# Moving one low-part subtraction from VectorE to GpSimd in the first group of a batched graph-attention kernel, and the point from which GpSimd's first sum may start

## The chip, the cores and the metric

The kernel runs on one core of one Trainium2 chip. The metric is the device time of one execution in microseconds (us). It was run three times before the change: 520.58, 521.08 and 521.65 us, median 521.08 us. The profile comes from a further execution that took 520.78 us.

## The reference, cut to what matters

For each of 32 batches, x is 256 x 512 and adj is 256 x 256; `weight`, `wq` and `wk` are 512 x 512 and shared by all batches.

```
output = x @ weight
q, k   = x @ wq, x @ wk
alpha  = max(q @ k^T, 0) * (adj != 0)
alpha  = softmax(alpha, axis=1)
out    = layernorm(x + alpha @ output)
```

All of it is float32.

## The kernel before, in words

**Splits.** TensorE multiplies a float32 matrix in three passes: each operand X is kept as a high part (`X_hi`, X rounded to the type TensorE reads) and a low part (`X_lo = X - X_hi`), and a product is hi·hi + lo·hi + hi·lo. `add_chunk` (lines 339 to 341) issues these three matmuls. ScalarE makes the high parts by a copy; VectorE or GpSimd makes the low parts by a subtraction.

**Algebra.** The score matrix is x (wq wk^T) x^T, so the kernel first computes G = wq wk^T once, and then for every batch T = G x^T, the scores from x and T, V = x W, and the softmax-weighted sum of V. T and V are made with a Strassen-like scheme of seven half-size products P1 to P7. Their left operands are the four blocks A11, A12, A21, A22 of x and four sums of blocks S1 to S4; their right operands are blocks of G (or W) and four sums T1, T2, T3, D4 of such blocks.

**Order of the work.** The batches go in pairs (16 of them), the pairs in groups of two called slot 0 and slot 1. `x_summed`, `s_hi_ready` and `s_lo_ready` are semaphores with one counter per slot. Groups 1 to 7 run in a rolled loop; the first group (pairs 0 and 1) is written out by hand, as are the queues of all engines. Each engine executes its own list strictly in order, so a waiting instruction holds all that stands behind it.

**The first group on TensorE** runs: 14 warm-up matmuls, `fill_g` (G), `fill_first_v` for three of four rows of V of pair 0, then `fill_first_t` (T of both pairs, products in the order P1, P2, P7, P6, P5, P3, P4, two halves each of six matmuls), the scores of pair 0 in two halves (`fill_first_s`), the last row of V, the scores of pair 1, and so on. `fill_first_v(0)` waits for the low parts of all four rows of W (`w_lo_ready`, count K = 4). P6 multiplies S2 by T2: it waits for the low part of T2 of G (`gt_lo_ready`, made by `split_gt(T2)` on VectorE), for the low part of S2 in both slots, and for the first copy of the chain bank. P5 waits for T1 and S1, P3 for S4. P3's first half also waits for ScalarE's copy of P5's first half (`t_copied` 5), and ScalarE's `copy_first_t(P5, 0)` in turn waits until GpSimd has made the low part of A22 of slot 1.

**VectorE in this stretch** makes the low parts of x of pair 0 (`split_x0`, four), of W (four), then the splits and sums of G, among them `split_first_s(0, S3)`, `split_first_b(A11)`, `split_first_b(A12)`, `split_first_s(1, S3)`, `split_gt(T3)`, `split_first_s(0, S2)`, `split_first_s(1, S2)`, `split_gt(T2)`, `split_first_v(2)`, `split_gt(T1)`, two sums of A11 and `split_gt(D4)`. The subtractions are all recorded at line 1110 (the helper `rest`).

**GpSimd in this stretch** makes the block sums S1 to S4 of both slots (`sum_first_x`, recorded at line 1527), the low parts of S1 and S4 of both slots (`split_first_s`, line 1531), the low parts of A22 and A21 of slot 1 (`split_first_a`, line 1536), and then the four sums of blocks of W (lines 1614 to 1622). Its first sum waits for the low parts of wq and wk, the second for `w_lo_ready`. Pair 0's sums lie in `xs`; pair 1's lie in parts of `parts` and `adj`, and SyncE loads the first adjacency matrix over the latter once the sums and low parts of S1 and S4 of slot 1 are done.

**ScalarE** makes the high parts in the order of its list: the high part of S3 of slot 0 (line 1000) stands directly behind the third split of G and ahead of A11 (line 993), the fourth split of G and `split_first_v(0)` (line 971).

Of the kernel before, what the change touches and what calls it, by code (L numbers as in the profile page):

```python
# [38 lines left out]
S1, S2, S3, S4 = range(4)  # L39
# [6 lines left out]
S_HI = ({S2: 1, S3: 2, S1: 3, S4: 4}, {S3: 1, S2: 2, S4: 3, S1: 4})  # L46
S_LO = ({S2: 1, S3: 2, S1: 3, S4: 4}, {S3: 1, S2: 2, S1: 3, S4: 4})

FIRST_A, FIRST_S = (A11, A12, A22, A21), (S3, S1, S2, S4)
FIRST_LO = {S3: 1, S2: 2}, {S1: 1, S4: 2}  # L50

T_HI = ({A11: 1, A22: 2, A12: 3, A21: 4}, {A11: 1, A12: 2, A21: 3, A22: 4})
T_LO = ({A11: 1, A22: 2, A12: 3, A21: 4}, {A11: 1, A12: 2, A22: 3, A21: 4})
# [12 lines left out]
def gnn_resnorm(nc: bass.Bass, x, x_t, adj_t, w, wq_t, wk_t, out):  # L66
# [3 lines left out]
    K = D // P  # L70
# [10 lines left out]
    with ExitStack() as ctx:  # L81
# [107 lines left out]
        w_hi_ready, w_lo_ready = sem("w_hi_ready"), sem("w_lo_ready")  # L189
# [8 lines left out]
        x_summed, s_hi_ready, s_lo_ready = sems("x_summed"), sems("s_hi_ready"), sems("s_lo_ready")  # L198
# [138 lines left out]
        def _(pe):  # L337
# [38 lines left out]
            def fill_t(i):  # L376
                def copy_taken(n):
                    pe.wait_ge(t_copied, COPIES * i + n)

                def sum_taken(n):  # L380
                    pe.wait_ge(t_summed, T_SUMS * i + n)

                def x_split(u):
                    pe.wait_ge(a_lo_ready[0], 4 * i + A_LO[0][u])
                    if u in B_LO_FIRST:
                        pe.wait_ge(b_lo_ready, 2 * i + B_LO_FIRST[u])
                    else:
                        pe.wait_ge(a_lo_ready[1], 2 * i + A_LO[1][u])

                def xs_split(s):  # L390
                    for slot in range(2):
                        pe.wait_ge(s_lo_ready[slot], 4 * i - 2 + S_LO[slot][s])

                both = slice(0, 2)
                xs_split(S3)
                t_half(P7, 0, both)

                pe.wait_ge(v_lo_ready, 8 * i - 4 + V_AT[1][A12])
                x_split(A11)
                t_half(P1, 0, both)  # L400
                t_half(P1, 1, both)

                pe.wait_ge(v_summed, V_SUMS * (2 * i - 2) + 2)
                x_split(A12)
                t_half(P2, 0, both)
                pe.wait_ge(v_summed, V_SUMS * (2 * i - 2) + 3)
                t_half(P7, 1, both)
                sum_taken(1)
                t_half(P2, 1, both)
                copy_taken(1)  # L410
                xs_split(S2)
                t_half(P6, 0, both)
                copy_taken(2)
                t_half(P6, 1, both)
                copy_taken(3)
                xs_split(S1)
                t_half(P5, 0, both)
                copy_taken(4)
                t_half(P5, 1, both)
                copy_taken(5)  # L420
                xs_split(S4)
                t_half(P3, 0, both)
                copy_taken(6)
                t_half(P3, 1, both)
                sum_taken(3)
                x_split(A22)
                t_half(P4, 0, both)
                sum_taken(4)
                t_half(P4, 1, both)

            def fill_first_t():

                def xs_split(s):
                    for slot in range(2):
                        if s in FIRST_LO[0]:
                            pe.wait_ge(first_s_lo_ready[slot], FIRST_LO[0][s])
                        else:
                            pe.wait_ge(s_lo_ready[slot], FIRST_LO[1][s])

                both = slice(0, 2)  # L440
                pe.wait_ge(g_lo_ready, 2)
                pe.wait_ge(b_lo_ready, B_LO_FIRST[A11])
                t_half(P1, 0, both)
                t_half(P1, 1, both)
                pe.wait_ge(g_lo_ready, 4)
                pe.wait_ge(gt_summed, 1)
                pe.wait_ge(b_lo_ready, B_LO_FIRST[A12])
                t_half(P2, 0, both)

                pe.wait_ge(v_lo_ready, 2)  # L450
                t_half(P2, 1, both, o_bank[0][:])
                pe.wait_ge(gt_lo_ready, G_ORDER.index(T3) + 1)
                xs_split(S3)

                pe.wait_ge(v_lo_ready, 1)
                t_half(P7, 0, both)

                pe.wait_ge(gt_summed, 8)
                t_half(P7, 1, both)
                pe.wait_ge(t_copied, 1)  # L460
                pe.wait_ge(gt_lo_ready, G_ORDER.index(T2) + 1)
                xs_split(S2)
                t_half(P6, 0, both)
                pe.wait_ge(t_copied, 2)
                t_half(P6, 1, both)
                pe.wait_ge(t_copied, 3)
                pe.wait_ge(gt_lo_ready, G_ORDER.index(T1) + 1)
                xs_split(S1)
                t_half(P5, 0, both)
                pe.wait_ge(t_copied, 4)  # L470
                t_half(P5, 1, both)
                pe.wait_ge(t_copied, 5)
                xs_split(S4)
                t_half(P3, 0, both)
                pe.wait_ge(t_copied, 6)
                t_half(P3, 1, both)
                pe.wait_ge(t_summed, 3)
                pe.wait_ge(gt_lo_ready, G_ORDER.index(D4) + 1)
                pe.wait_ge(a_lo_ready[1], A_LO[1][A22])
                t_half(P4, 0, both)  # L480
                pe.wait_ge(t_summed, 4)
                t_half(P4, 1, both)
# [625 lines left out]
        def _(dve):  # L1108
# [237 lines left out]
            def split_first_s(slot, s):  # L1346
                dve.wait_ge(s_hi_ready[slot], FIRST_S.index(s) + 1)
                rest(s_lo[:, slot, s], xs[:, s] if slot == 0 else xs1_raw[s], s_hi[:, slot, s]).then_inc(first_s_lo_ready[slot], 1)
# [48 lines left out]
            sum_gt(D4, 1)  # L1397
            split_first_v(1)
            split_gt(T3)
            split_first_s(0, S2)  # L1400
            split_first_s(1, S2)
            split_gt(T2)
            split_first_v(2)
# [106 lines left out]
        @block.gpsimd  # L1510
        def _(pool):
            def first_sum_split(slot, s):
                if s in FIRST_LO[0]:
                    pool.wait_ge(first_s_lo_ready[slot], FIRST_LO[0][s])
                else:
                    pool.wait_ge(s_lo_ready[slot], FIRST_LO[1][s])

            def sum_first_x(slot, s):
                xb = {u: xt[:, u] for u in range(4)} if slot == 0 else x1_raw
                xs_to = {u: xs[:, u] for u in range(4)} if slot == 0 else xs1_raw  # L1520
                for u in {S3: (A11, A21), S1: (A22,), S2: (), S4: (A12,)}[s]:
                    pool.wait_ge((x0_loaded if slot == 0 else x1_loaded)[u], 16)
                if s in (S2, S4):
                    pool.wait_ge(x_summed[slot], S_SUMMED[s] - 1)
                a, b, op = {S3: (xb[A11], xb[A21], ALU.subtract), S1: (xb[A21], xb[A22], ALU.add),
                            S2: (xs_to[S1], xb[A11], ALU.subtract), S4: (xb[A12], xs_to[S2], ALU.subtract)}[s]
                nc.gpsimd.tensor_tensor(xs_to[s], a, b, op).then_inc(x_summed[slot], 1)

            def split_first_s(slot, s):
                pool.wait_ge(s_hi_ready[slot], FIRST_S.index(s) + 1)  # L1530
                nc.gpsimd.tensor_tensor(s_lo[:, slot, s], xs[:, s] if slot == 0 else xs1_raw[s], s_hi[:, slot, s].bitcast(F32),
                                        ALU.subtract).then_inc(s_lo_ready[slot], 1)
# [6 lines left out]
            def sum_x(i, slot, s, first=False):  # L1539
                for u in {S3: (A11, A21), S1: (A22,), S2: (), S4: (A12,)}[s]:  # L1540
                    pool.wait_ge(xt_loaded[u], 32 * i + 16 * slot - 16)

                if not first:
                    pool.wait_ge(s_lo_ready[1 - slot], 4 * i - 6 + 4 * slot + S_LO[1 - slot][s])
                else:
                    first_sum_split(0, s)
                if s in (S2, S4):
                    pool.wait_ge(x_summed[slot], 4 * i + S_SUMMED[s] - 1)
                a, b, op = {S3: (xt[:, A11], xt[:, A21], ALU.subtract), S1: (xt[:, A21], xt[:, A22], ALU.add),
                            S2: (xs[:, S1], xt[:, A11], ALU.subtract), S4: (xt[:, A12], xs[:, S2], ALU.subtract)}[s]  # L1550
                nc.gpsimd.tensor_tensor(xs[:, s], a, b, op).then_inc(x_summed[slot], 1)  # L1551
# [40 lines left out]
            nc.gpsimd.memset(minus_half[:], -0.5).then_inc(half_ready, 1)  # L1592
            pool.wait_ge(half_ready, 1)

            pool.wait_ge(qk_lo_ready, 2 * K)
            sum_first_x(0, S3)

            pool.wait_ge(w_lo_ready, K)
            sum_first_x(0, S1)
            sum_first_x(1, S3)  # L1600
            sum_first_x(0, S2)
            sum_first_x(1, S1)
            sum_first_x(1, S2)
            split_first_s(0, S1)
            split_first_s(1, S1)
            sum_first_x(0, S4)
# [79 lines left out]
```

## Time and profile before

| what | value |
|---|---|
| runs before, us | 520.58, 521.08, 521.65 (median 521.08) |
| profiled execution, us | 520.78 |
| its span, us | 519.0 |
| granted TensorE clock, mean over the span | 0.997 of full |
| TensorE busy | 98% of the span |
| VectorE, ScalarE, GpSimd busy | 73%, 64%, 51% |

The span is the time from the first to the last instruction of the profiled execution; the remaining 1.78 us of it lie around the span. Times in the rows are counted from the start of the span. PE is TensorE's matmuls, PEld its weight loads, DVE is VectorE, ACT is ScalarE, POOL is GpSimd, SPq is SyncE's queue, which issues DMAs. A matmul's duration overlaps its follower's, so the pace of TensorE is read from the distance of two starts.

### The profile page before, as it was taken

To read this page: it belongs to the slowest core of one execution; us is meant where nothing else is said; L and a number is where in the kernel's file an instruction comes from. 1 tells how busy PE (TensorE), PEld (TensorE's weight loads), DVE (VectorE), ACT (ScalarE), POOL (GpSimd) and SP (SyncE) were. 2 spreads that over 40 slices of the span, in tenths; PEclk is the share of its full clock that TensorE was granted. 3 is DMA by queue.
4 is the path that set the end of the run, shared out by engine and by line. 5 is a ranking of instruction groups with operands and counts; after the bars stand their busy time and mean duration, and the time that the engine had idled before them with its cause. 6 is when DMAs were issued, how large, how long until landed. Compare 5 with 4: busy or idle time off the path is not lost.

```text
span 519.0 us, 9822 instructions
## 1 busy us (share of the span) xinstructions
PE 510.6 (98%) x3206; PEld 464.0 (89%) x3206; DVE 379.1 (73%) x744; ACT 330.9 (64%) x756; POOL 263.4 (51%) x199
## 2 busy tenths in 40 slices
PE   8999999999999999999999999999999999999995
PEld 7779998899989998899988999889998999889994
DVE  6997855776848677586866778577684866757586
ACT  6855756386763857649474586638676385764677
POOL 1799884339535377145651486433953537610011
PEclk9999999999999999999999999999999999999998
DMA  8412151044520626025350342405342061501426
GB/s 291 175 61 83 67 182 58 20 124 163 178 84 20 221 62 242 20 61 182 116 203 20 125 139 110 175 20 151 132 179 84 20 222 61 202 1 35 168 90 235
DMA packets 30367, 62.05 MB, mean 120 GB/s; under 512 B 2064, under 2 KB 2320, under 8 KB 30352
## 3 DMA queue, kind: packets, MB, share of 16 engines
q1 hardware_dynamic: 30064, 61.48, 34.7%
q10 hardware_dynamic: 288, 0.39, 0.2%
q8 instruction: 7, 0.11, 0.1%
q14 instruction: 8, 0.07, 0.0%
HBM read 45.09 MB, written 16.78 MB: 119 GB/s over the span
## 4 chain that ended last, share of the span: by engine, by line
PE 95%; DMA 1%; SPq 1%; DVE 1%; issue 1%; ACT 0%; POOLq 0%; POOL 0%; DVEq 0%; ACTq 0%
PE o_bank L339 12%; PE o_bank L340 12%; PE o_bank L341 12%; PE chain L339 11%; PE chain L341 11%; PE chain L340 11%; PE bank_y L339 6%; PE bank_y L340 6%; PE bank_y L341 6%; PE bank_z L341 3%; PE bank_z L340 3%; PE bank_z L339 3%; DMA xn<-in_w 1%; SPq L293 0%; SPq L289 0%
## 5 line engine op out<-in xcount | busy, mean ns | idle before, releaser
L1560 POOL TENSOR_TENSOR s_lo<-xs,s_hi 128x512 fp32r<-128x512 f32 x56 | 76.4, 1378 | 36.7 <-ACT s_hi L727 36.7
L1555 POOL TENSOR_TENSOR a_lo<-xt,a_hi 128x512 fp32r<-128x512 f32 x42 | 57.5, 1375 | 61.3 <-ACT a_hi L719 61.3
L339 PE MATMUL o_bank<-t_hi,a_hi 128*128 128x256 f32 x256 | 72.5, 283 | 0.0
L340 PE MATMUL o_bank<-t_lo,a_hi 128*128 128x256 f32 x256 | 72.4, 283 | 0.0
L341 PE MATMUL o_bank<-t_hi,a_lo 128*128 128x256 f32 x256 | 72.4, 283 | 0.0
L1565 POOL TENSOR_TENSOR rstd<-var_eps,minus_half 128x4 f32<-128x4 f32 x14 | 14.2, 1017 | 92.6 <-DVE var_eps L1202 92.6
L750 ACT COPY parts<-chain 128x256 f32<-128x256 f32 x90 | 33.2, 369 | 43.3 <-PE chain L341 42.1
L1122 DVE TENSOR_TENSOR parts<-parts,bank_y 128x512 f32<-128x512 f32 x32 | 22.0, 688 | 41.9 <-ACT parts L736 25.8
L1551 POOL TENSOR_TENSOR xs<-xt 128x512 f32<-128x512 f32 x28 | 36.8, 1325 | 27.9 <-DMA xt<-in_x_t 27.9
L339 PE MATMUL chain<-w_hi,s_hi 128*128 128x256 f32 x180 | 50.9, 283 | 0.0
L340 PE MATMUL chain<-w_lo,s_hi 128*128 128x256 f32 x180 | 50.9, 283 | 0.0
L341 PE MATMUL chain<-w_hi,s_lo 128*128 128x256 f32 x180 | 50.9, 283 | 0.0
L1188 DVE SCALAR_TENSOR_TENSOR xn<-o_bank,xn 128x512 f32<-128x512 f32 x62 | 42.4, 684 | 10.2 <-PE o_bank L341 10.1
L339 PEld LDWEIGHTS o_bank<-t_hi,a_hi 128*128 128x128 f32 x256 | 49.1, 192 | 0.4
L340 PEld LDWEIGHTS o_bank<-t_lo,a_hi 128*128 128x128 f32 x256 | 49.1, 192 | 0.4
L341 PEld LDWEIGHTS o_bank<-t_hi,a_lo 128*128 128x128 f32 x256 | 49.1, 192 | 0.0
L339 PE MATMUL o_bank<-v_hi,p_hi 128*128 128x512 f32 (+1 forms) x126 | 49.0, 389 | 0.1
L340 PE MATMUL o_bank<-v_lo,p_hi 128*128 128x512 f32 (+1 forms) x126 | 48.9, 388 | 0.0
L341 PE MATMUL o_bank<-v_hi,p_lo 128*128 128x512 f32 (+1 forms) x126 | 48.8, 387 | 0.0
L1110 DVE TENSOR_TENSOR v_lo<-parts,v_hi 128x512 fp32r<-128x512 f32 x45 | 46.8, 1052 | 0.1
L1208 DVE TENSOR_SCALAR xn<-xn,neg_mean,rstd 128x512 f32<-128x512 f32 x56 | 39.3, 723 | 10.1 <-POOL rstd L1565 10.1
L778 ACT CAST t_hi<-parts 128x512 fp32r<-128x512 f32 x24 | 14.8, 621 | 49.8 <-PE o_bank L341 49.8
(209 smaller groups left out, 1648.6 us busy)
## 6 DMA issues: line engine op xcount, KB each, us to landing
xn<-in_x SPq DMA_DIRECT2D x16, 1024.0 KB, 5.2
xt<-in_x_t SPq DMA_DIRECT2D x60, 256.0 KB, 3.1
out<-xn SPq DMA_DIRECT2D x14, 1024.0 KB, 5.3
adj<-in_adj_t SPq DMA_DIRECT2D x16, 512.0 KB, 4.8
xn<-in_wq_t SPq DMA_DIRECT2D x4, 256.0 KB, 4.0
xn<-in_w SPq DMA_DIRECT2D x4, 256.0 KB, 6.9
out<-xn SPq DMA_DIRECT2D x2, 512.0 KB, 3.1
parts<-in_wk_t SPq DMA_DIRECT2D x3, 256.0 KB, 4.5
```

The lines of the kernel that those rows point to most:

```text
L339: nc.tensor.matmul(dst, a[0], b[0], start=first, stop=False, skip_group_check=shared)
L340: nc.tensor.matmul(dst, a[0], b[1], start=False, stop=False, skip_group_check=shared)
L341: return nc.tensor.matmul(dst, a[1], b[0], start=False, stop=last, skip_group_check=shared)
L750: nc.scalar.copy(parts[:, PART[product], c, 0], chain_v[:, c]).then_inc(v_copied, 1)
L778: nc.scalar.copy(t_hi[:, u], whole).then_inc(t_hi_ready, 1)
L1110: return nc.vector.tensor_tensor(dst, whole, hi.bitcast(F32), ALU.subtract)
L1122: nc.vector.tensor_tensor(part, part, bank, ALU.add).then_inc(t_summed, 1)
L1188: nc.vector.scalar_tensor_tensor(out=xn[:, slot, r], in0=row.rearrange("q j n -> q (j n)"), scalar=1.0, in1=xn[:, slot, r], op0=ALU.mult, ...
L1208: nc.vector.tensor_scalar(xn[:, slot, r], xn[:, slot, r], neg_mean[:, r:r + 1], rstd[:, r:r + 1], ALU.add, ALU.mult).then_inc(normed, 1)
L1551: nc.gpsimd.tensor_tensor(xs[:, s], a, b, op).then_inc(x_summed[slot], 1)
L1555: nc.gpsimd.tensor_tensor(a_lo[:, slot, u], xt[:, u], a_hi[:, slot, u].bitcast(F32), ALU.subtract).then_inc(a_lo_ready[slot], 1)
L1560: nc.gpsimd.tensor_tensor(s_lo[:, slot, s], xs[:, s], s_hi[:, slot, s].bitcast(F32), ALU.subtract).then_inc(s_lo_ready[slot], 1)
```

## The change: what it does

- VectorE no longer makes the low part of S2 of slot 0 (`split_first_s(0, S2)` leaves its list). GpSimd makes it, behind its sum S2 of slot 1 and ahead of its low part of S1 of slot 0.
- GpSimd's wait for the low parts of W stands ahead of its first sum (S3 of slot 0) and no longer behind it; the wait for the low parts of wq and wk goes.
- The counts follow: in slot 0 GpSimd now signals three low parts in the first group and VectorE one; `S_LO_LESS` corrects the counts that the loop waits for.

```diff
-FIRST_LO = {S3: 1, S2: 2}, {S1: 1, S4: 2}
+FIRST_LO_DVE = {S3: 1}, {S3: 1, S2: 2}
+FIRST_LO_POOL = {S2: 1, S1: 2, S4: 3}, {S1: 1, S4: 2}
+
+S_LO_LESS = (1, 2)
...
-                        pe.wait_ge(s_lo_ready[slot], 4 * i - 2 + S_LO[slot][s])
+                        pe.wait_ge(s_lo_ready[slot], 4 * i - S_LO_LESS[slot] + S_LO[slot][s])
...
-                        if s in FIRST_LO[0]:
-                            pe.wait_ge(first_s_lo_ready[slot], FIRST_LO[0][s])
+                        if s in FIRST_LO_DVE[slot]:
+                            pe.wait_ge(first_s_lo_ready[slot], FIRST_LO_DVE[slot][s])
                         else:
-                            pe.wait_ge(s_lo_ready[slot], FIRST_LO[1][s])
+                            pe.wait_ge(s_lo_ready[slot], FIRST_LO_POOL[slot][s])
...
             split_gt(T3)
-            split_first_s(0, S2)
             split_first_s(1, S2)
             split_gt(T2)
...
                 if not first:
-                    pool.wait_ge(s_lo_ready[1 - slot], 4 * i - 6 + 4 * slot + S_LO[1 - slot][s])
+                    pool.wait_ge(s_lo_ready[1 - slot],
+                                 4 * (i - 1 + slot) - S_LO_LESS[1 - slot] + S_LO[1 - slot][s])
...
-            pool.wait_ge(qk_lo_ready, 2 * K)
+            pool.wait_ge(w_lo_ready, K)
             sum_first_x(0, S3)
-
-            pool.wait_ge(w_lo_ready, K)
             sum_first_x(0, S1)
             sum_first_x(1, S3)
             sum_first_x(0, S2)
             sum_first_x(1, S1)
             sum_first_x(1, S2)
+            split_first_s(0, S2)
             split_first_s(0, S1)
             split_first_s(1, S1)
```

## Rows read from the trace of the kernel before

**Rows 1.** The page, busy time and share of the span by engine.

```profile
PE 510.6 (98%) x3206; PEld 464.0 (89%) x3206; DVE 379.1 (73%) x744; ACT 330.9 (64%) x756; POOL 263.4 (51%) x199
```

**Rows 2.** Windows: length, then PE, PEld, DVE, ACT, POOL busy, PE's clock, DMA.

```profile
16.50:17.50 1.00, 0.90 (x5) 0.43 (x4) 1.00 (x3) 1.00 (x4) 0.41 (x1) 1.00 0.15 57
17.50:33.00 15.50, 15.50 (x70) 12.82 (x69) 15.50 (x21) 11.17 (x22) 15.42 (x11) 1.00 0.21 69
33.00:35.00 2.00, 0.82 (x5) 0.39 (x4) 2.00 (x3) 0.00 (x0) 2.00 (x2) 1.00 0.00 0
49.50:507.00 457.50, 457.50 (x2958) 419.72 (x2958) 330.87 (x670) 292.08 (x685) 227.56 (x170) 1.00 0.33 113
```

**Rows 3.** Timeline of PE: start us, duration us, line, operation, idle time before.

```profile
16.57 0.39 PE L341 MATMUL bank_y<-s_hi,t_lo 128*128 128x512 f32 x1
17.06 0.50 PE L339 MATMUL bank_y<-w_hi,a_hi 128*128 128x512 f32 x1
17.40 0.39 PE L340 MATMUL bank_y<-w_lo,a_hi 128*128 128x512 f32 x1
...
33.29 0.39 PE L341 MATMUL bank_y<-s_hi,g_lo 128*128 128x512 f32 x1
34.86 0.47 PE L339 MATMUL chain<-s_hi,g_hi 128*128 128x512 f32 x1 [1.18 <-issue]
35.17 0.39 PE L340 MATMUL chain<-s_lo,g_hi 128*128 128x512 f32 x1
...
48.61 0.28 PE L341 MATMUL o_bank<-t_hi,a_lo 128*128 128x256 f32 x1
48.75 0.39 PE L339 MATMUL o_bank<-t_hi,a_hi 128*128 128x256 f32 x1
48.98 0.28 PE L340 MATMUL o_bank<-t_lo,a_hi 128*128 128x256 f32 x1
```

**Rows 4.** The chain that ended last, in order of time: start, duration, engine.

```profile
14.82 0.62 ACT w_hi L1017
...
16.33 0.69 DVE w_lo L1110
```

**Rows 5.** Timeline of DVE.

```profile
29.59 1.78 DVE L1110 TENSOR_TENSOR s_lo<-xs,s_hi 128x512 fp32r<-128x512 f32 x1
31.29 1.78 DVE L1110 TENSOR_TENSOR s_lo<-parts,s_hi 128x512 fp32r<-128x512 f32 x1
33.00 1.76 DVE L1110 TENSOR_TENSOR g_lo<-xn,g_hi 128x512 fp32r<-128x512 f32 x1
34.68 0.68 DVE L1110 TENSOR_TENSOR v_lo<-o_bank,v_hi 128x512 fp32r<-128x512 f32 x1
...
47.51 1.19 DVE L1110 TENSOR_TENSOR t_lo<-parts,t_hi 128x512 fp32r<-128x512 f32 x1 [0.69 <-ACT t_hi L762]
```

**Rows 6.** Timeline of POOL.

```profile
11.72 1.72 POOL L1527 TENSOR_TENSOR xs<-xt 128x512 f32<-128x512 f32 x1 [10.89 <-DMA xt<-in_x_t]
17.09 1.30 POOL L1527 TENSOR_TENSOR xs<-xt 128x512 f32<-128x512 f32 x1 [3.64 <-DVE w_lo L1110]
18.35 1.29 POOL L1527 TENSOR_TENSOR parts<-soft 128x512 f32<-128x512 f32 x1
...
24.38 1.79 POOL L1531 TENSOR_TENSOR s_lo<-xs,s_hi 128x512 fp32r<-128x512 f32 x1
...
34.17 1.73 POOL L1536 TENSOR_TENSOR a_lo<-parts,a_hi 128x512 fp32r<-128x512 f32 x1
...
46.85 1.30 POOL L1551 TENSOR_TENSOR xs<-xs,xt 128x512 f32<-128x512 f32 x1
```

**Rows 7.** DVE from 12.24 us on, in narrow windows of the timeline.

```profile
12.24 1.76 DVE L1110 TENSOR_TENSOR a_lo<-xt,a_hi 128x512 fp32r<-128x512 f32 x1
```

**Rows 8.** Timeline of ACT.

```profile
20.12 0.59 ACT L971 CAST v_hi<-bank_y 128x512 fp32r<-128x512 f32 x1 [1.56 <-PE bank_y L341]
...
39.34 0.59 ACT L745 COPY parts<-chain 128x512 f32<-128x512 f32 x1 [0.33 <-PE chain L341]
```

**Rows 9.** Timeline of SP.

```profile
34.28 0.33 SPq L307 DMA_DIRECT2D adj<-in_adj_t  x1
```

**Rows 10.** Timeline of DVE, the first mask.

```profile
49.03 0.69 DVE L1161 SCALAR_TENSOR_TENSOR soft<-adj,o_bank 128x512 f32<-128x512 int32 x1 [0.33 <-PE o_bank L341]
```

More of the change, by code:

```diff
@@ L1512, in first_sum_split @@
             def first_sum_split(slot, s):
-                if s in FIRST_LO[0]:
-                    pool.wait_ge(first_s_lo_ready[slot], FIRST_LO[0][s])
+                if s in FIRST_LO_DVE[slot]:
+                    pool.wait_ge(first_s_lo_ready[slot], FIRST_LO_DVE[slot][s])
                 else:
-                    pool.wait_ge(s_lo_ready[slot], FIRST_LO[1][s])
+                    pool.wait_ge(s_lo_ready[slot], FIRST_LO_POOL[slot][s])
             def sum_first_x(slot, s):
```

## The prediction

> **What bounds the kernel now.** I read the page first: TensorE is busy for 98% of the span, every other engine for 73% or less [rows 1]. So a microsecond is worth something only where TensorE stands still. The windows show where: TensorE is busy without a break from 49.5 to 507 us and from 17.5 to 33.0, but has only 0.82 of the 2.00 us from 33 to 35, and 0.90 of the one at 16.5 [rows 2]. The granted clock is 1.00 in all four, so no level of the clock is at stake.
>
> The timeline of TensorE gives the prices. Undisturbed, matmuls on 512 columns start 0.227 us apart (from 17.40 to 33.29 are 70 steps, 15.89 us; the count is that of the second window [rows 2]). Three places break the pace [rows 3]:
> - At 16.57 the last matmul of G starts. The next two are due at 16.80 and 17.02 and come at 17.06 and 17.40: **0.38 us** lost, wait and restart together.
> - At 33.29 the last matmul of P7 starts. The next two are due at 33.52 and 33.74 and come at 34.86 and 35.17: **1.43 us** lost.
> - At 48.61, on 256 columns with a pace of 0.12, the two behind it come at 48.75 and 48.98 instead of 48.73 and 48.85: **0.13 us** lost.
>
> Who ends them? For the first, the chain names VectorE's last low part of W, 16.33 to 17.02 [rows 4]. The second is labelled "issue", which names nobody; but P6 waits for the low part of T2, and VectorE makes that from 33.00 to 34.76 [rows 5], 0.10 before P6 starts. The third waits for the low part of T's block A21, which ends at 48.70 [rows 5].
>
> The rows also show why VectorE is late. A subtraction whose operands are all in SBUF takes 1.76 to 1.78 us, one with its operand in a PSUM bank (34.68) takes 0.68 [rows 5]. GpSimd's instructions show the mirror image: 1.30 us at 17.09, 1.72 to 1.79 at 11.72, 24.38 and 34.17 [rows 6]. The two alternate: where both queues are full, each pair takes 1.70 us (distance of starts 29.59, 31.29, 33.00), about 1.15 for GpSimd and 0.55 for VectorE. So an SBUF subtraction costs VectorE 1.70 us of its queue here, and adds 0.45 to GpSimd, whose own pace is 1.26 (17.09 to 18.35).
>
> **Part 1: the first sum waits.** GpSimd's sum at 11.72 runs beside VectorE's four low parts of x; the third of those, at 12.24, takes 1.76 [rows 7] where 0.68 would do. With the sum gone from there the four end 1.1 us earlier. VectorE's low parts of W then follow ScalarE, whose last high part of W ends at 14.82 + 0.62 = 15.44 [rows 4]. The last low part runs from about 15.47 to 16.15 instead of 16.33 to 17.02: 0.87 earlier. TensorE needs it at 16.80, so the first stall goes whole: **minus 0.38**. What is late next: nothing, G itself paces TensorE. ScalarE now has to wait for S3: GpSimd starts it at about 16.23, it ends at 17.53, and ScalarE's high part of S3 stood ready for it at 16.9. ScalarE so loses 0.65 us, covered by its idle 1.56 before the high part of V at 20.12 [rows 8], which comes 0.38 earlier itself: 0.5 is left over. Cost 0. No DMA is issued earlier or later by this but those below.
>
> **Part 2: VectorE's queue.** The low part of T2 is the eighth SBUF subtraction of VectorE behind W and becomes the seventh. From 34.76 go 1.70 for the one removed and 0.87 for the earlier start: 32.2. TensorE wants P6 at 33.52 - 0.38 = 33.14, so T2 must land by 33.04. It does, by 0.8: **minus 1.43**. The rows leave one doubt. Which engine goes first when both are ready within 0.05 us decides whether VectorE waits for one GpSimd instruction more, 1.15 us, and my walk meets three such ties (about 23.5, 27.0 and 28.0). One lost tie puts T2 at 33.3, P6 at 33.4, and takes back 0.2 plus a restart of 0.08. I take none lost, as the nearest rows alternate evenly; 0.28 is the bound for the range.
>
> **Part 3: GpSimd's queue.** It takes two instructions more behind 16.23. Check of the price on before: from 17.09 to 35.90, the end of A22's low part (34.17 + 1.73), 12 instructions and 8 alternations, 12 x 1.26 + 8 x 0.45 = 18.7 against 18.8 measured. After: 14 instructions, 8 or 9 alternations, 21.2 to 21.7 us, so A22 ends at 37.5 to 37.9, 1.6 to 2.0 later than before. Who waits for what stands in that queue:
> - S2's low part itself, now seventh, ends at 16.23 + 7 x 1.26 + 4 x 0.45 = 26.9; P6 wants it at 33.14. Free.
> - The low part of S4 of slot 1 ends at about 36.2; P3 wants it at 38.6. The adjacency load behind it on SyncE, issued at 34.28 [rows 9], moves to 36.3; the mask that needs it runs at 49.03 [rows 10]. Free; the load behind it waits for later events.
> - A22: ScalarE's copy of P5's first half, at 39.34 [rows 8] and due at 37.5 after the shift, waits for it. P3 is 24 steps behind P6, at 33.14 + 5.45 = 38.6. If A22 ends at 37.9, the copy (0.59 long) ends at 38.55. Free, but only just; 0.1 at the bound.
> - The sums of W and what follows come 1 to 1.5 us later. ScalarE's splits of W have 3 us of cover. But they lie differently beside VectorE: the low part of A21 of T, at 47.51, waited there for a GpSimd instruction that ran 46.85 to 48.15 [rows 5, 6]. Free it would take 0.68 and end 0.5 early; behind a GpSimd instruction just begun it ends 0.6 late. Today it costs 0.13. The bounds are 0 and 0.7, I take **0.28, which is 0.15** more than today, since GpSimd is busy there without a break.
>
> **Sum.** 0.38 + 1.43 - 0.15 = 1.66 us. From 49.5 us on TensorE has no idle stretch [rows 2] and the other engines follow it, so the whole shift reaches the end. The profiled execution would go from 520.78 to 519.12. It lies 0.30 below the median of the runs, so against the median 521.08 the sum gives 519.4; half of the ties' 0.28 is a fair allowance, and I say 519.5. A measurement of this kernel can tell about 0.2%, 1.04 us, from no change.
>
> **A rule against the change.** VectorE's subtraction alone takes 0.68 us, GpSimd's alone 1.30 [rows 5, 6]. The Trainium skill (GPSIMD Engine Reference, Engine selection) sends elementwise work on a tile to VectorE and calls GpSimd about twice as slow with two inputs. By that rule the move swaps a cheap instruction for one of twice its price; the trace agrees on the bare ratio, 1.9. The sum goes by the 1.70 us of queue instead, because both queues are full there.
>
> **The rivals.**
> 1. *VectorE gains only the bare price.* If the removed subtraction is worth its pace alone, 0.60, and the earlier start is eaten by the later sums, T2 lands at 34.16 and P6 starts at 34.26: 0.60 plus 0.38 gained, less 0.15. Gain 0.8, 520.3. Against it stand the 1.70 steps. Chance 0.07.
> 2. *The ties fall badly.* 0.28 lost at P6, 0.1 at P3, and 0.7 instead of 0.13 at 48.7: 1.81 - 0.28 - 0.1 - 0.57 = 0.86, 520.2; with two of the three, gain 1.1. For it: nothing fixes the phases. Chance 0.20, half of it under 1.04 us.
> 3. *Slower: GpSimd's queue becomes the bound.* Place: ScalarE's copy of P5's first half behind A22's low part. P3 then starts 0.69 after A22 ends, so it costs from 37.9 on and eats the whole gain from 39.7 on. If all 14 instructions take the 1.79 of 24.38, A22 ends at 41.3, P3 is 3.4 late, and the kernel is 1.6 slower: 522.7. Against it: VectorE has only nine SBUF subtractions in that time. Chance 0.05.
> 4. *It does not do what it says*: P6 is held by something else ("issue" names nobody), and only the first stall goes: 520.7. Against it: the 0.10 between T2's end and P6. Chance 0.05.
>
> **How the numbers follow.** Forecast, a gain of 1.2 to 1.95: 0.60. Rivals 0.07, 0.20, 0.05, 0.05; 0.03 is left for small gains of other kinds. Faster by over 0.2%: 0.60 + 0.10 = 0.70. Within: 0.07 + 0.10 + 0.05 + 0.03 = 0.25. Slower 0.05. Range: below, a gain of 1.94 (no third stall at all) and 0.3 for the scatter of the runs, 518.9; above, rivals 1 and 2 with the same scatter, 520.6. It leaves out rivals 3 and 4.
>
> **What would show it.** Right: TensorE steps evenly through 16.8; VectorE's last low part of W starts near 15.5; T2 ends at 32 to 33.1; no gap in TensorE ahead of P6; A22's low part ends before 38; scores of pair 0 start near 44.1 instead of 45.86. Wrong: T2 ends behind 33.1, a gap ahead of P3 near 38.6, or one of over 0.5 us between the two halves of the scores near 47.

## The result, and the profile after

The changed kernel is slower: 523.93 us (median of 7 runs, 522.59 to 524.51) against 521.04 us (7 runs) of the kernel before, ratio 1.005 with an interval of 1.0036 to 1.0065. The forecast was 519.5, range 518.9 to 520.6. The profiled execution has a span of 522.6 us against 519.0.

The stall ahead of P6 is gone. V starts 0.54 us earlier, though behind a longer stall (0.80 us against 0.38), and two small new stalls came; all that is over by 48 us. What decides comes later. The timeline of TensorE after the change (start, duration, line, operation, idle time before), to be held against [rows 3]:

```profile
15.60 0.39 PE L345 MATMUL bank_y<-s_hi,t_lo 128*128 128x512 f32 x1
16.52 0.50 PE L343 MATMUL bank_y<-w_hi,a_hi 128*128 128x512 f32 x1 [0.53 <-DVE w_lo L1114]
...
35.47 0.39 PE L345 MATMUL chain<-s_hi,g_lo 128*128 128x512 f32 x1
35.97 0.50 PE L343 MATMUL chain<-s_hi,g_hi 128*128 128x512 f32 x1
...
38.59 0.39 PE L345 MATMUL chain<-s_hi,g_lo 128*128 128x512 f32 x1
39.20 0.50 PE L343 MATMUL chain<-s_hi,g_hi 128*128 128x512 f32 x1 [0.21 <-ACT parts L749]
...
58.95 0.28 PE L345 MATMUL o_bank<-t_hi,a_lo 128*128 128x256 f32 x1
62.17 0.50 PE L343 MATMUL o_bank<-v_hi,p_hi 128*128 128x512 f32 x1 [2.94 <-DVE v_lo L1114]
62.51 0.39 PE L344 MATMUL o_bank<-v_lo,p_hi 128*128 128x512 f32 x1
62.74 0.45 PE L345 MATMUL o_bank<-v_hi,p_lo 128*128 128x512 f32 x1
62.99 0.63 PE L343 MATMUL o_bank<-v_hi,p_hi 128*128 128x512 f32 x1
63.42 0.63 PE L344 MATMUL o_bank<-v_lo,p_hi 128*128 128x512 f32 x1
```

Between 58.95 and 62.17 TensorE waits 3.1 us for the low part of V's last row. Then its matmuls stand 0.43 apart instead of 0.23. The windows (length, busy time of PE, PEld, DVE, ACT, POOL, then the granted clock) say that this is the clock, granted at 0.81 and then at 0.50 of full:

```profile
59.10:62.20 3.10, 0.15 (x3) 0.03 (x1) 3.10 (x4) 1.53 (x3) 3.10 (x3) 1.00 0.00 0
62.20:63.40 1.20, 1.20 (x4) 0.98 (x5) 1.20 (x3) 0.00 (x0) 1.20 (x2) 0.81 0.00 0
63.40:66.00 2.60, 2.60 (x8) 2.01 (x7) 1.88 (x10) 1.09 (x4) 2.60 (x3) 0.50 0.52 162
70.00:510.00 440.00, 440.00 (x2845) 403.76 (x2845) 314.88 (x633) 279.70 (x654) 212.28 (x157) 1.00 0.33 113
```

In the first two of these windows VectorE and GpSimd are both busy without a break. VectorE after the change, the four low parts of P of pair 0 (line 1182) and then the one that TensorE waits for:

```profile
54.12 1.69 DVE L1114 TENSOR_TENSOR t_lo<-parts,t_hi 128x512 fp32r<-128x512 f32 x1
55.74 1.52 DVE L1182 SCALAR_TENSOR_TENSOR p_lo<-soft,inv_sum,p_hi 128x256 fp32r<-128x256 f32 x1
57.18 1.52 DVE L1182 SCALAR_TENSOR_TENSOR p_lo<-soft,inv_sum,p_hi 128x256 fp32r<-128x256 f32 x1
58.62 1.50 DVE L1182 SCALAR_TENSOR_TENSOR p_lo<-soft,inv_sum,p_hi 128x256 fp32r<-128x256 f32 x1
60.04 1.48 DVE L1182 SCALAR_TENSOR_TENSOR p_lo<-soft,inv_sum,p_hi 128x256 fp32r<-128x256 f32 x1
61.44 0.68 DVE L1114 TENSOR_TENSOR v_lo<-o_bank,v_hi 128x512 fp32r<-128x512 f32 x1
```

The same instructions in the kernel before, which the prediction did not read:

```profile
55.08 0.66 DVE L1110 TENSOR_TENSOR t_lo<-parts,t_hi 128x512 fp32r<-128x512 f32 x1
55.87 1.30 DVE L1178 SCALAR_TENSOR_TENSOR p_lo<-soft,inv_sum,p_hi 128x256 fp32r<-128x256 f32 x1
57.10 0.47 DVE L1178 SCALAR_TENSOR_TENSOR p_lo<-soft,inv_sum,p_hi 128x256 fp32r<-128x256 f32 x1
57.49 0.47 DVE L1178 SCALAR_TENSOR_TENSOR p_lo<-soft,inv_sum,p_hi 128x256 fp32r<-128x256 f32 x1
57.89 0.47 DVE L1178 SCALAR_TENSOR_TENSOR p_lo<-soft,inv_sum,p_hi 128x256 fp32r<-128x256 f32 x1
58.29 0.68 DVE L1110 TENSOR_TENSOR v_lo<-o_bank,v_hi 128x512 fp32r<-128x512 f32 x1
```

GpSimd beside them, in the kernel before:

```profile
52.77 1.75 POOL L1625 TENSOR_TENSOR w_lo<-xn,w_hi 128x512 fp32r<-128x512 f32 x1
55.42 1.46 POOL L1560 TENSOR_TENSOR s_lo<-xs,s_hi 128x512 fp32r<-128x512 f32 x1 [0.90 <-ACT s_hi L727]
58.03 1.50 POOL L1560 TENSOR_TENSOR s_lo<-xs,s_hi 128x512 fp32r<-128x512 f32 x1 [1.14 <-ACT s_hi L727]
```

and after the change:

```profile
55.23 1.75 POOL L1628 TENSOR_TENSOR w_lo<-xn,w_hi 128x512 fp32r<-128x512 f32 x1
56.93 1.48 POOL L1564 TENSOR_TENSOR s_lo<-xs,s_hi 128x512 fp32r<-128x512 f32 x1
58.38 1.46 POOL L1564 TENSOR_TENSOR s_lo<-xs,s_hi 128x512 fp32r<-128x512 f32 x1
59.79 1.44 POOL L1628 TENSOR_TENSOR w_lo<-xn,w_hi 128x512 fp32r<-128x512 f32 x1
```

Before, GpSimd stood idle for 0.90 and 1.14 us in this stretch, waiting for ScalarE. In the second pause three of the four low parts of P ran at 0.47 us each. After, GpSimd comes later: its low part of W, the one ahead of the first pause, starts at 55.23 instead of 52.77. TensorE and VectorE come some 1 us earlier (the last matmul ahead of the wait starts at 58.95 instead of 60.11). So both pauses are filled, and each low part of P waits for one GpSimd instruction, at 1.5 us. The four last 5.78 us from start to end instead of 2.49.

The differences add up, with a gap taken as what stands above the pace of 0.227 (0.119 on 256 columns): V starts at 16.52 instead of 17.06, -0.54; P6, -1.42; new ahead of P5, +0.37; new ahead of P3, +0.48; the low part of T's A21, -0.11; the wait near 59, 3.10 and 0.11 for its restart, +3.21; eight matmul steps at the lower clock (62.99 to 66.38), +1.57. Sum +3.56, and the spans differ by 3.6.

### The profile page after: what moved, and what is told of

The parts are those of the page before. It is cut to its first block, busy times and chain, and to the rows that moved or that the text cites. A ratio compares the mean times of both kernels' runs of the same rounds, so it can differ in the third digit from the quotient of the medians.

```text
span 522.6 us, 9802 instructions
## 1 busy us (share of the span) xinstructions
PE 511.9 (98%) x3206; PEld 464.5 (89%) x3206; DVE 380.1 (73%) x743; ACT 331.0 (63%) x756; POOL 267.4 (51%) x200
## 4 chain that ended last, share of the span: by engine, by line
PE 86%; DVE 1%; issue 0%; POOLq 0%; POOL 0%; ACT 0%; DVEq 0%; ACTq 0%
PE o_bank L343 11%; PE o_bank L344 11%; PE o_bank L345 11%; PE chain L344 10%; PE chain L345 10%; PE chain L343 10%; PE bank_y L344 5%; PE bank_y L343 5%; PE bank_y L345 5%; PE bank_z L344 3%; PE bank_z L345 3%; PE bank_z L343 3%; DVE p_lo L1182 0%; DVE xn L1460 0%; DVE xn L1192 0%
## 5 line engine op out<-in xcount | busy, mean ns | idle before, releaser
L1126 DVE TENSOR_TENSOR parts<-parts,bank_y 128x512 f32<-128x512 f32 x32 | 21.9, 687 | 42.6 <-ACT parts L740 25.8
L1114 DVE TENSOR_TENSOR v_lo<-parts,v_hi 128x512 fp32r<-128x512 f32 x45 | 48.8, 1096 | 0.1
L740 ACT COPY parts<-chain 128x512 f32<-128x512 f32 x42 | 24.6, 587 | 34.7 <-PE chain L345 34.2
```

The lines of the kernel that those rows point to most:

```text
L740: nc.scalar.copy(parts[:, PART[product], c], chain[:, c]).then_inc(t_copied, 1)
L1114: return nc.vector.tensor_tensor(dst, whole, hi.bitcast(F32), ALU.subtract)
L1126: nc.vector.tensor_tensor(part, part, bank, ALU.add).then_inc(t_summed, 1)
```

## The experiments

All times are medians of runs beside the kernel before on the same chip, with the ratio and its interval.

**1 and 2: GpSimd holds still during the low parts of P.** In the changed kernel, and as a control in the kernel before.

```diff
             for b in W_ORDER[:-1]:
+                if b == T2:
+                    pool.wait_ge(p_lo_ready, R)
                 split_wt(b)
```

Expected of the first:

> The changed kernel, but GpSimd waits for the low parts of P of pair 0 (p_lo_ready = 4) ahead of its low part of W's T2, so that nothing of GpSimd runs beside those four VectorE instructions. Theory A (GpSimd's queue, moved 1 to 2 us later and without its two idle gaps, runs beside VectorE's four low parts of P and makes each take 1.5 us where 0.68 would do; TensorE then waits for the low part of V's last row, and its clock falls): the four take about 2.5 us in all where they took 5.8, TensorE has no gap near 59 us and no stretch at half clock, and the time is that of before less the 1.1 us gained until then, 519.5 to 520.3. Theory B (the time is lost elsewhere, for instance in the loop or in transfers that start later, and the gap near 59 us is only where it shows): another wait takes the gap's place, 522.5 to 524.5.

Of the control:

> The kernel before with the same hold of GpSimd ahead of its low part of W's T2. Theory A: the four low parts of P take 2.5 us in the kernel before already, so the hold gains nothing; its own cost is nothing either, if GpSimd's later instructions have cover: 520.8 to 521.3. If the hold by itself were worth a microsecond, a good result of the first run would not speak for theory A.

Measured: 523.55 (ratio 1.0054, 1.0033 to 1.0076) and 522.79 (1.0042, 1.0028 to 1.0056). Theory A's time failed in both runs; the first lies in theory B's range, 522.5 to 524.5. The traces say why. The first wait is gone: in run 1 the four low parts of P take 1.66 us from start to end and no gap stands near 59 us. But the hold keeps GpSimd still for 2.22 us (4.81 in the control, where 2.04 were idle before), and TensorE meets GpSimd again at the start of the second group. TensorE in the changed kernel with the hold:

```profile
74.64 0.28 PE L345 MATMUL bank_y<-w_hi,a_lo 128*128 128x256 f32 x1
77.53 0.50 PE L343 MATMUL bank_y<-s_hi,g_hi 128*128 128x512 f32 x1 [2.61 <-POOL s_lo L1564]
```

and GpSimd there:

```profile
68.88 1.29 POOL L1559 TENSOR_TENSOR a_lo<-xt,a_hi 128x512 fp32r<-128x512 f32 x1
70.13 1.30 POOL L1555 TENSOR_TENSOR xs<-xt 128x512 f32<-128x512 f32 x1
...
74.53 1.27 POOL L1555 TENSOR_TENSOR xs<-xt 128x512 f32<-128x512 f32 x1 [3.10 <-DMA xt<-in_x_t]
75.76 1.71 POOL L1564 TENSOR_TENSOR s_lo<-xs,s_hi 128x512 fp32r<-128x512 f32 x1
```

The last low part of x of pair 2 ends at 70.17; the block of pair 3 is loaded over it only then; the sum S1 waits for that load until 74.53; and the low part of S3, which P7 wants, stands behind that sum. So GpSimd's whole queue of the first group has little slack. Another wait took the gap's place, as theory B said, so these two runs do not decide between the theories; run 5 does.

**5 and 6: the low part of S3 goes ahead of the sum that waits**, with the hold and without it.

```diff
             sum_x(1, 1, S3)
-            sum_x(1, 1, S1)
             split_s(1, 1, S3)
+            sum_x(1, 1, S1)
             sum_x(1, 1, S2)
```

> The changed kernel with the hold of the first run, and with GpSimd's low part of S3 of slot 1 for the second group moved ahead of its sum S1 of that slot, which waits for a transfer. Theory A (two places, both GpSimd's queue: the low parts of P near 57 us, and behind the hold the low part of S3 that stands behind the sum waiting for x of pair 3): both gaps go, TensorE has none between 48 and 505 us, and the time is that of before less what was gained until 48 us: 519.8 to 520.5. Theory B (GpSimd's queue is too full anywhere in the first group): a third wait appears in the second group, 521.5 or more.

> The changed kernel with only the low part of S3 moved ahead of the sum S1, without the hold. Theory A: the low parts of P are slowed as before, the wait of 3 us near 59 us stays, and the move is worth nothing there: 522.6 to 524.5, as the changed kernel.

Measured: with the hold 520.07 (ratio 0.9988, 0.9979 to 0.9997), without it 524.42 (1.0067, 1.0052 to 1.0082). With both edits the two waits are gone; only 0.42 us near 81 us stays between 48 and 506, and no third wait of theory B's kind comes. The swap by itself does nothing for the wait near 59 us, which is 3.1 us again. Between 5 and 6 the hold is the only difference, and it is worth over 4 us (524.42 against 520.07). This is what shows that GpSimd's instructions beside the low parts of P cost the time.

**3 and 4: each part of the change alone.** Run 3 keeps the old start of the first sum, run 4 leaves the low part of S2 on VectorE.

```diff
# run 3, against the changed kernel
-            pool.wait_ge(w_lo_ready, K)
+            pool.wait_ge(qk_lo_ready, 2 * K)
             sum_first_x(0, S3)
+
+            pool.wait_ge(w_lo_ready, K)
             sum_first_x(0, S1)
# run 4, against the kernel before: the reverse of these lines
```

> Only the low part of S2 of slot 0 goes to GpSimd; the first sum starts as before, ahead of the low parts of W. Theory A: the low part of T2 ends 1.7 earlier, at 33.1, TensorE is about 1.3 ahead at 50 us, and GpSimd 0.8 behind, which together is as much as its idle 0.90 and 1.14 us near 55 and 57; so most of the four low parts of P are slowed, TensorE waits 1 to 3 us for the last row of V: 520.5 to 523. Theory B: nothing of it near 59 us, 519.7.

> Only the wait moves: GpSimd's first sum starts behind the low parts of W; VectorE keeps the low part of S2. Theory A: both queues start 0.9 earlier, TensorE gains 0.4 at 17 us and up to 0.9 ahead of P6; GpSimd is 0.4 behind, so some 0.4 us of its idle time is left near 55 us, and one or two low parts of P are slowed: TensorE waits 0 to 1.5 us, 519.8 to 521.5. Theory B: 519.8.

Measured: 525.23 (1.0079, 1.0062 to 1.0095) and 524.94 (1.0063, 1.0043 to 1.0082). Each alone is as slow as both. In both traces all four low parts of P take 1.5 us, and TensorE waits over 3 us. Run 4 was expected to wait 1.5 us at most, with GpSimd 0.4 us behind. GpSimd in run 4:

```profile
54.07 1.75 POOL L1623 TENSOR_TENSOR w_lo<-xn,w_hi 128x512 fp32r<-128x512 f32 x1
55.78 1.74 POOL L1560 TENSOR_TENSOR s_lo<-xs,s_hi 128x512 fp32r<-128x512 f32 x1
57.62 1.35 POOL L1560 TENSOR_TENSOR s_lo<-xs,s_hi 128x512 fp32r<-128x512 f32 x1
```

GpSimd was further behind than 0.4. Its first sum starts at 16.63, only 0.46 ahead of where its second stood before, and it meets VectorE once more on the way: its low part of A22 ends at 37.16 instead of 35.90, and its low part of W at 55.82 instead of 54.52, 1.30 later. VectorE's instruction in front of the low parts of P, at 54.67 instead of 55.08, now starts beside that low part of W and takes 1.70 instead of 0.66; by the time the low parts of P come, ScalarE has GpSimd's next operand ready and no pause is left for them. So what was wrong is the size of GpSimd's delay. What a delay of 0.4 us would do, this run does not show. From 1.30 us here to 2.46 in the changed kernel the loss does not grow: TensorE waits 3.1 us in both.

Run 4 also shows that the new wait alone does not help P6: the low part of T2 ends 0.45 earlier, at 34.31, and the stall ahead of P6 is 1.46 us, as long as before. Run 3 also showed what the first sum's early start saves: no stall ahead of P5 or P3, but 0.95 us between 44 and 49 us.

**7 and 8: a dose in the kernel before.** One subtraction more on GpSimd, ahead of the sums of W, 512 or 192 columns wide; its result is overwritten unread. Nothing else is touched.

```diff
+            pool.wait_ge(xt_loaded[A11], 16)
+            pool.wait_ge(xt_loaded[A12], 16)
+            nc.gpsimd.tensor_tensor(p_lo[:, 0:M], xt[:, A11], xt[:, A12], ALU.subtract)
             pool.wait_ge(w_lo_ready, K)
```

> The kernel before with one more subtraction of 128 x 512 on GpSimd, 1.26 us, ahead of its sums of W; its result is read by nobody. Nothing else is changed, VectorE's and TensorE's lists are those of before. Theory A: a GpSimd queue 1.26 us later loses its idle 0.90 us near 55, runs beside the low parts of P without a break, and slows two to four of them from 0.47 to 1.5 us; the last row of V has 1.2 us of slack, so TensorE waits 1 to 2.5 us near 60 us: 522 to 525. Theory B (the loss needs the change's other parts): 521.2.

> The same with 128 x 192, some 0.5 us. Theory A, as a dose: 0.5 us stays within the idle 0.90 us near 55, GpSimd's low part of S2 starts where it did, one low part of P is slowed as before, and the time is that of before: 520.9 to 521.6. If 0.5 us brings the whole wait, the idle time is not what protects the low parts of P.

Measured: 525.48 (1.0087, 1.0072 to 1.0103) and 521.41 (1.0007, 0.9998 to 1.0016). One instruction of 1.26 us on an engine that is busy for half of the span costs 4.6 us; the short one costs nothing that is clear of noise. VectorE with the wide one:

```profile
55.18 1.69 DVE L1110 TENSOR_TENSOR t_lo<-parts,t_hi 128x512 fp32r<-128x512 f32 x1
56.79 1.52 DVE L1178 SCALAR_TENSOR_TENSOR p_lo<-soft,inv_sum,p_hi 128x256 fp32r<-128x256 f32 x1
...
62.50 0.68 DVE L1110 TENSOR_TENSOR v_lo<-o_bank,v_hi 128x512 fp32r<-128x512 f32 x1
```

and with the narrow one:

```profile
55.65 0.66 DVE L1110 TENSOR_TENSOR t_lo<-parts,t_hi 128x512 fp32r<-128x512 f32 x1
56.45 1.30 DVE L1178 SCALAR_TENSOR_TENSOR p_lo<-soft,inv_sum,p_hi 128x256 fp32r<-128x256 f32 x1
57.67 0.47 DVE L1178 SCALAR_TENSOR_TENSOR p_lo<-soft,inv_sum,p_hi 128x256 fp32r<-128x256 f32 x1
```

VectorE's and TensorE's lists are those of the kernel before in both, so in run 7 GpSimd's lateness alone brings the whole effect.

Run 8 is no clean dose. GpSimd's low part of W starts 0.58 us later (53.35), but its pauses stay 0.90 and 1.13 us, although 0.90 less 0.58 would be 0.32. The reason lies ahead of them: VectorE's low part of T's block A21 met a GpSimd instruction just begun, and TensorE lost 0.66 us there instead of 0.13.

```profile
47.54 1.73 DVE L1110 TENSOR_TENSOR t_lo<-parts,t_hi 128x512 fp32r<-128x512 f32 x1 [0.69 <-ACT t_hi L762]
```

TensorE, ScalarE and VectorE then run 0.57 later as well (VectorE's instruction at 55.65 instead of 55.08), so beside them GpSimd is as early as in the kernel before. The run therefore does not show that a delay of half a microsecond is harmless to the low parts of P, and no run here has a delay against VectorE between that of the kernel before and those of runs 4 and 7.

**9 to 11: versions that might beat both.** Run 9 is run 3 with the hold and the swap. Run 10 is run 5 with the hold one instruction later:

```diff
             for b in W_ORDER[:-1]:
                 split_wt(b)
+            pool.wait_ge(p_lo_ready, R)
             split_s(1, 0, S2)
```

Run 11 is run 10 with A22 of slot 1 split earlier on ScalarE and GpSimd.

```diff
# ScalarE
+            split_first_a(A22)
+            split_first_a(A21)
             split_first_s(0, S4)
             split_first_s(1, S4)
-            split_first_a(A22)
-            split_first_a(A21)
# GpSimd
+            split_first_a(A22)
             split_first_s(1, S4)
-            split_first_a(A22)
             split_first_a(A21)
```

> The third run's kernel (only S2's low part moved; the first sum starts ahead of W's low parts) with the hold and the earlier low part of S3. Theory A: no gap near 59 us and none near 75; what stays is the first stall (0.4) and the two at 44 and 47 us (0.2 and 0.7) that the third run showed: 519.9 to 520.6. It tells what the first sum's wait is worth once GpSimd's queue no longer decides.

> As the fifth run, but the hold stands one instruction later, behind the low part of W's T2: GpSimd stands idle for about 1 us instead of 2.2, one or two of the low parts of P run beside it. The last row of V has 1.2 us of slack or more, so TensorE should have no gap near 59 us, and the stall of 0.42 us near 81 us goes if it comes from GpSimd being late: 519.6 to 520.3.

> As the tenth, and A22 and A21 of slot 1 are split earlier: their high parts ahead of those of S4 on ScalarE, where it stood idle for 3 us, and GpSimd's low part of A22 ahead of that of S4 of slot 1. Theory: the stalls of 0.37 and 0.48 us ahead of P5 and P3 come from ScalarE's and GpSimd's late A22; both go or shrink, unless the low part of S4 of slot 1, now last, is late for P3 itself (a stall near 38 us of up to 0.8): 519.0 to 520.0.

Measured: 520.20 (0.9988, 0.9979 to 0.9997), 519.60 (0.9978, 0.9969 to 0.9987) and 519.86 (0.9978, 0.9969 to 0.9987). Run 10 has the lowest median, 1.36 us under the kernel before: nearly the gain that was forecast for the change, had with one more wait and one line moved. Its interval overlaps those of runs 5, 9 and 11, so it is not shown to be better than they are. GpSimd stands still for 1.55 us in it, one low part of P takes 1.51 and no gap comes near 59 us; of the stall near 81 us 0.1 is left. Its windows, TensorE first:

```profile
16.00:48.00 32.00, 31.76 (x154) 26.23 (x153) 27.13 (x36) 19.90 (x39) 31.62 (x21) 1.00 0.28 90
48.00:505.80 457.80, 457.80 (x2960) 419.76 (x2958) 330.95 (x670) 292.72 (x685) 233.57 (x172) 1.00 0.33 113
```

Run 11 took away the stall ahead of P5 and left 0.34 ahead of P3, but TensorE then waited 0.70 us near 47 us for a low part of T; the sum is unchanged. Run 9 against run 5 (ratio 0.9988 in both) says that the first sum's wait is worth nothing that these runs can tell.

## Why the prediction was wrong, step by step

- **What bounds the kernel**: right. TensorE's three stalls and who ends them were read rightly; the low part of T2 held P6, since the stall goes in the changed kernel and in run 3.
- **Part 1**: right in kind, its size varies. The last low part of W ended at 16.46, 0.55 earlier than before and not 0.87. The stall ahead of V is 0.37 to 1.05 us in the six profiles without the new wait (before, runs 2, 3, 7, 8, 9); of the seven with it, it is gone in four (5, 6, 10, 11) and 0.31, 0.56 and 0.80 in the others (4, 1, after). The 0.80 comes with a G that ended 0.97 earlier than before; in that execution ScalarE also waited 0.41 us in the middle of its high parts of x for a load, which it had not done in the profile before.
- **Part 2**: right. T2 was to land at 32.2 and ended at 32.58 (30.81 + 1.77 in the trace); P6 starts without a stall, 1.42 gained for 1.43 forecast. No tie fell badly. The removed subtraction did this alone: run 3 has no stall there either, and run 4 keeps it.
- **Part 3, A22**: a size off. It was to end at 37.5 to 37.9 and ended at 38.48 (the first sum started at 16.60 instead of 16.23, and the 14 instructions took 21.9 us instead of 21.2 to 21.7), so the copy of P5's first half, and with it P3, were late by 0.48; rival 3's place, at a seventh of its price. A second stall, 0.37 ahead of P5, was not foreseen: ScalarE's copies stood behind its high parts of S4 and A22, which waited for GpSimd's sums.
- **Part 3, "the sums of W and what follows"**: this is the step that failed. It followed GpSimd's queue to the low part of T's A21, put 0.15 us down for it, and stopped at 48.7 us; what lies behind was taken at nothing. The measured price of that was 3.21 us of waiting and 1.57 of lower clock in the profile. Seven microseconds on, VectorE has four more instructions with all tensors in SBUF, and GpSimd's pauses of 0.90 and 1.14 us were what let them run at 0.47. The price of an alternation was known from [rows 5]; it was applied to the instructions that the change moves and not to all that GpSimd's later queue would meet. At 48.7 itself nothing was lost in the changed kernel, where 0.28 was forecast; the other end of the forecast's bounds, 0.7, came in runs 3, 8, 9 and 11 (0.66 to 0.74).
- **Sum, "the whole shift reaches the end"**: wrong for the same reason. That TensorE had no idle stretch from 49.5 us on [rows 2] says that nothing was late, not by how much. The last row of V had 1.2 us of slack (58.97 against the 60.2 at which TensorE came to it), GpSimd's low part of S3 for the second group about as little; run 2 shows the latter, with a stall of 1.39 us at 76 us in an otherwise unchanged kernel.
- **Rule against the change**: the Trainium skill (GPSIMD Engine Reference, Engine selection) was right to speak against it, though not by its reason. The double price of the one instruction, 1.26 for 0.60, was hidden; what cost 4.8 us in the profile was that GpSimd's queue as a whole came later. Another page of the Trainium skill (SBUF — State Buffer, SBUF: two separate sides) calls the port pair that VectorE and GpSimd share an exclusive lock, held for a whole instruction. The trace agrees: a low part of P lasts 0.47 alone and 1.5 when a GpSimd instruction, itself 1.30 alone, has begun.
- **Rivals**: the slower case had 0.05 and the right engine, but its place, its price and its condition were others. The forecast's chance of 0.70 for faster was far too high, because every bad case that was priced lay ahead of 49 us.

## What to carry to other kernels

When work goes to an engine with idle time, look at what its idle moments protect: follow its whole queue until it really waits long enough to catch up, and list at each point which instructions of the other engine need both inputs from SBUF. Give the slack of every consumer, not only the stalls that exist. If the pauses matter, make them on purpose: one wait that keeps GpSimd still for VectorE's critical instructions, with the work that TensorE needs soonest moved ahead of waits for transfers. Both belong together: the wait alone lost time (runs 1 and 2), and so did the moved line alone (run 6). When a dose is given to an engine, look in the trace whether the others moved with it, before reading a small effect as harmless.

## What the runs showed of the hardware that was not expected

- The engine with the short instructions bears nearly all of the alternation. The same four VectorE instructions take 2.49 us in all in the kernel before (1.30, 0.47, 0.47, 0.47) and 5.78 us in the changed kernel and in run 7 (1.48 to 1.52 each), while GpSimd's beside them take 1.44 to 1.48 (changed kernel) where they take 1.30 alone. The loss did not grow with GpSimd's delay: 5.78 us in the changed kernel and in run 4 too. Where it sets in was not measured.
- A wait of 3.1 us cost more than itself. In the profile TensorE's clock stood at 0.50 of full, 1.2 GHz, from 63.4 to 66.0 us, though it ran matmuls again since 62.17. The runs of the changed kernel fall into two groups with the mean clock over the span: 522.59, 522.70 and 523.34 at 0.997, and 523.93 to 524.51 at 0.994 or 0.995, so in four of seven a further 1.4 us (the means of the groups) went with it. In the profiles of runs 1 and 3, waits of 2.9 and 3.3 us were followed by no such stretch, but other executions of both fall into the same two groups: in run 1 522.68 to 522.79 at 0.999 or 1.000, and 524.32 to 526.17 at 0.990 to 0.996; in run 3 523.74 at 0.997, and 525.09 to 525.38 at 0.994 or 0.995. As far as the mean clock tells, the same wait is followed by the lower clock in some executions and not in others.
